# Perceiver attention by pairs of batches: scores, exponentials, turns and copies in half slots

## The chip, the cores and the metric

The kernel runs on one core of one Trainium2 chip. The metric is the device time of one execution in microseconds (us). The time before is the median of three runs, 2326.81 us (2326.65 to 2334.06).

## What is computed

The program is one block of a network with eight layers over x, 32 batches of 128 rows of 128 numbers, all in float32. The change touches the fifth layer (layer 4), an attention of the perceiver kind. Each batch attends to 128 context rows (of 96 numbers) and to its own 128 rows, with 2 heads of 64:

```python
xn = layernorm(x, ln_x_g, ln_x_b)            # x: the context here
ln = layernorm(latents, ln_l_g, ln_l_b)      # latents: layernorm of the resident x
q = ln @ Wq.T
kv = jnp.concatenate([xn @ Wkv.T, ln @ Wlkv.T], axis=1)
k, v = (kv[..., :INNER], kv[..., INNER:])
qn = rmsnorm(q, qn_g) * SCALE                # per head
kn = rmsnorm(k, kn_g)
attn = jnp.einsum('bhid,bhjd->bhij', qn, kn)
attn = jnp.where(full_mask[:, None, None, :], attn, -jnp.finfo(attn.dtype).max)
attn = jax.nn.softmax(attn, axis=-1)
out = jnp.einsum('bhij,bhjd->bhid', attn, v)
out = out.transpose(0, 2, 1, 3).reshape(b, m, INNER)
return out @ Wo.T + bo                       # times tanh(gate), added to x
```

## The kernel before

The layers run one after another with a barrier between them; x stays in SBUF (`x_resident`). Layer 4 is `layer4_perceiver` (line 1656). Its 32 batches go in 8 groups of G = 4. Each engine has its own program, a loop over slots t from -4 to 8, written out, and executes it strictly in the order of the text; semaphores with counts hold the engines together. In slot t the groups are at different steps: group t+4 has its statistics taken, t+3 is normalised and turned (work bank, copied out by ScalarE, ACT), t+2 is projected to q, k and v (`project`, lines 1951 to 1959, kept by `keep`, 1863) and squared (`square`, 1869), t+1 has its mean squares, roots (GpSimd, POOL, 1731 and 1733), scaled keys (1773) and its q, k_lat and k_ctx turned, t has scores (1961), mask, maximum and shift (`mask_scores`, 1779) and exponentials (`exponentiate`, 1887), and t-1 has its probabilities turned (1943), copied (1856), weighed with v (1975), scaled by the sums (1803), turned, mixed with wo (2024) and added to x (`update`, 1811).

PSUM is full: `score_bank` is four banks of 512 columns, in which both the scores of a group and later its turned probabilities lie (batch b's turned probabilities in bank b, a pair's scores in two banks, one for each head); `project_bank` is two, `work_bank` and `out_bank` one each. Before the change, `scores(t)` waits until all four turned probabilities of t-1 are copied, `mask_scores(t)` does both halves of the scores and then both maxima and gives one shift, and `exponentiate(t)` does the eight exponentials (two heads, four batches) at the end of ACT's slot. TensorE (PE) turns the probabilities first in slot t+1. VectorE (DVE) begins a slot by the reciprocal of the sums (1801), which waits for the exponentials, and the mean squares (1761), which wait for `square`.

## Time and profile before

| | |
|---|---|
| median of 3 runs | 2326.81 us |
| profiled execution, time | 2330.86 us |
| profiled execution, span | 2329.1 us |
| PE, DVE, ACT, POOL busy over the span | 87%, 68%, 54%, 34% |
| layer 4 in the trace | about 1358.7 to 1577.0 us |
| busy in layer 4: PE, DVE, ACT, POOL | 160.3, 115.8, 120.4, 69.1 us |

The profile is of one execution. Busy time is the time in which an engine executes; register, branch and semaphore instructions don't count. Matmuls are pipelined, so their rows overlap and their sum overstates the work: a step from one start to the next tells more. The granted clock is that of PE, 1.00 for 2.4 GHz and 0.50 for 1.2. The timeline merges like instructions that follow each other into one row.

### The profile page before, as it was taken

What the parts mean: (1) busy time and instruction counts of PE and PEld (TensorE: products, weight loads), DVE (VectorE), ACT (ScalarE), POOL (GpSimd) and SP (SyncE); (2) the same over time, 40 slices, a digit from 0 to 9 for tenths busy, and PEclk for the clock granted to TensorE, in tenths of its full rate; (3) what the DMA queues carried; (4) which work ended last, traced back from release to release, by engine and by line L of the source; (5) the groups of instructions that cost most, each with busy time, mean ns of one, the idle gap of its engine ahead of it and who ended that gap; (6) DMA issues with size and microseconds to landing.
All of it is one profiled execution on the core that took longest, in us unless ns stands there. A gap on an engine that the chain in (4) does not pass through costs nothing. (4 is left out here: it accounts for less than half of the span.)

```text
span 2329.1 us, 49606 instructions
## 1 busy us (share of the span) xinstructions
PE 2023.1 (87%) x18068; PEld 1531.8 (66%) x18068; DVE 1574.3 (68%) x3198; ACT 1254.5 (54%) x2840; POOL 796.4 (34%) x698
## 2 busy tenths in 40 slices
PE   6669999999996989789999967784998899999964
PEld 3359989899984666556666645664674566666654
DVE  5689999999997988645445356545465665656644
ACT  3279888888861767523332226741343566656631
POOL 1124444444461333234444443311000333333333
PEclk7579999999997999989999978985898899999975
DMA  2100000000002000055345300001000000000001
GB/s 58 42 1 8 14 9 14 15 8 15 13 3 76 9 9 5 16 111 112 73 96 124 74 18 11 1 1 52 1 0 11 1 4 5 5 5 5 1 2 37
DMA packets 41414, 61.75 MB, mean 27 GB/s; under 512 B 9464, under 2 KB 18208, under 8 KB 40800
## 3 DMA queue, kind: packets, MB, share of 16 engines
q1 hardware_dynamic: 41184, 58.66, 10.4%
q8 instruction: 148, 2.42, 0.4%
q14 instruction: 82, 0.67, 0.1%
HBM read 56.02 MB, written 2.62 MB: 25 GB/s over the span
## 5 line engine op out<-in xcount | busy, mean ns | idle before, releaser
L827 POOL TENSOR_TENSOR a_probs<-a_probs,a_rsums 128x1024 f32<-128x1024 f32 x64 | 121.3, 1896 | 322.6 <-DVE a_rsums L875 322.6
L1504 POOL TENSOR_TENSOR f_h<-f_gated,f_w_spread 128x512 f32<-128x512 f32 x128 | 161.6, 1268 | 196.8 <-DVE f_gated L1558 93.8
L1558 DVE TENSOR_TENSOR f_gated<-f_silu,f_up 128x512 f32<-128x512 f32 x128 | 87.2, 686 | 184.4 <-PE f_up L1635 169.8
L2330 ACT ACTIVATE f_combine<-f_logits,f_neg_row_max 128x128 f32<-128x128 f32 x512 | 198.4, 395 | 0.5 <-DVE f_neg_row_max L2188 0.5
L1598 ACT ACTIVATE f_silu<-f_gate 128x512 f32<-128x512 f32 x128 | 76.2, 597 | 222.7 <-PE f_gate L1635 220.3
L2149 POOL TENSOR_TENSOR f_slot_sum<-f_slot_sum,f_logits 128x512 f32<-128x512 f32 x96 | 122.6, 1277 | 182.7 <-DVE f_slot_max L2267 94.8
L1650 PEld LDWEIGHTS f_acc<-f_down,f_h 128*128 128x128 f32 x1024 | 129.5, 192 | 42.0 <-issue 37.2
L2157 POOL TENSOR_TENSOR f_acc<-f_acc,f_row_factor 128x512 f32<-128x512 f32 x128 | 136.3, 1066 | 60.6 <-DVE f_slot_max L2267 38.5
L2391 PE MATMUL f_give_bank<-f_y,f_combineT 128*128 128x128 f32 x1024 | 140.1, 280 | 12.1 <-DVE f_y L2237 7.5
L863 DVE TENSOR_REDUCE a_negmax<-a_score_bank 128x8 f32<-128x1024 f32 x64 | 78.2, 1223 | 103.4 <-PE a_score_bank L1004 103.4
L2380 PE MATMUL f_slot_bank<-f_logits,f_xn 128*128 128x128 f32 x1024 | 137.4, 277 | 6.4 <-issue 5.4
L2418 PE MATMUL f_logit_bank<-f_phi,f_xT 128*128 (+1 forms) x1024 | 137.6, 280 | 3.8 <-ACT f_logits L2310 3.8
L2391 PEld LDWEIGHTS f_give_bank<-f_y,f_combineT 128*128 128x128 f32 x1024 | 125.2, 193 | 19.8 <-DVE f_y L2237 13.4
L1635 PE MATMUL f_gate<-f_xT,f_gate_up 128*128 128x512 f32 x256 | 134.7, 608 | 2.1 <-DVE f_gated L1558 2.0
L2253 DVE TENSOR_TENSOR f_logits<-f_logits,f_neg_slot_max 128x512 f32<-128x512 f32 x128 | 132.5, 1035 | 4.0 <-ACT f_combine L2330 3.4
L1650 PE MATMUL f_acc<-f_down,f_h 128*128 128x128 f32 x1024 | 132.4, 276 | 2.0 <-POOL f_h L1504 2.0
L1635 PE MATMUL f_up<-f_xT,f_gate_up 128*128 128x512 f32 x256 | 131.9, 597 | 0.0
L2380 PEld LDWEIGHTS f_slot_bank<-f_logits,f_xn 128*128 128x128 f32 x1024 | 125.3, 193 | 8.2 <-issue 6.7
L2418 PEld LDWEIGHTS f_logit_bank<-f_phi,f_xT 128*128 128x128 f32 x1024 | 127.6, 197 | 4.4 <-ACT f_logits L2310 4.3
L2368 PE MATMUL f_expert_bank<-f_w,f_slots 128*32 128x128 f32 x4096 | 127.5, 276 | 1.2 <-issue 1.2
L2368 PEld LDWEIGHTS f_expert_bank<-f_w,f_slots 128*32 128x32 f32 x4096 | 109.6, 111 | 9.5 <-issue 1.9
L931 ACT ACTIVATE a_probs<-a_probs 128x1024 f32<-128x1024 f32 x64 | 67.8, 1060 | 72.3 <-DVE a_probs L866 72.3
(325 smaller groups left out, 5044.7 us busy)
## 6 DMA issues: line engine op xcount, KB each, us to landing
f_w_spread<-f_routing_rows SPq DMA_DIRECT2D x64, 512.0 KB, 10.1
f_w<-in_f_w SPq DMA_DIRECT2D x16, 256.0 KB, 2.5
a_cT<-in_ctxT SPq DMA_DIRECT2D x16, 192.0 KB, 2.5
f_gate_up<-in_f_guT SPq DMA_DIRECT2D x1, 2048.0 KB, 7.9
out<-x_resident SPq DMA_DIRECT2D x8, 256.0 KB, 2.4
c_cT<-in_ctxT SPq DMA_DIRECT2D x8, 192.0 KB, 2.4
a_ctx<-in_ctx SPq DMA_DIRECT2D x8, 192.0 KB, 2.5
f_phi<-in_f_phi SPq DMA_DIRECT2D x1, 1024.0 KB, 5.3
```

What stands on the lines that cost most here:

```text
L827: nc.gpsimd.tensor_tensor(probs[:, u], probs[:, u], rsums[:, u, :].unsqueeze(2).to_broadcast([S, 8, S]), ALU.mult).then_inc(normalised, 1)
L1504: nc.gpsimd.tensor_tensor(h[:, u % KEPT, :], gated[:, u % 2, :], w_spread[:, u // PER, u % PER, :], ALU.mult).then_inc(weighted, 1)
L1635: nc.tensor.matmul(ps[step % 2][:, :], gu_w[:, step, k, :], norm.xT[:, s, :], start=True, stop=True).then_inc(done, 1)
L1650: last = nc.tensor.matmul(acc[s][:, j * D:(j + 1) * D], h[:, u % KEPT, j * S:(j + 1) * S], down_w[:, u, :], start=u == 0 and j == 0, stop= ...
L2149: nc.gpsimd.tensor_tensor(slot_sum[:, :, :], slot_sum[:, :, :] if g > 1 else raw[:, (m - 1) % RING], raw[:, m % RING], ALU.add).then_inc(p ...
L2157: nc.gpsimd.tensor_tensor(acc[:, group(g), :], acc[:, group(g), :], factor[:, m // GROUPS % 3, group(g)].unsqueeze(2).to_broadcast([S, G, D]),
L2253: nc.vector.tensor_tensor(e, e, wide(neg_slot[:, m // GROUPS % 3, :]), ALU.add).then_inc(shifts, 1)
L2330: last = nc.scalar.activation(back[:, m % BACKS, j, :], raw[:, m % RING, j, :], ACT.Exp, bias=neg_row[:, k, b:b + 1], accum_out=row_part[: ...
L2368: last = nc.tensor.matmul(expert_banks[m % 2][rows, j * D:(j + 1) * D], slots[:, m % KEPT, j, rows], w_s[:, k, e, :], start=True, stop=True)
L2380: last = nc.tensor.matmul(slot_bank[:, j * CH:(j + 1) * CH], xn[:, g * G + j, :], raw[:, m % RING, j, :], start=True, stop=True)
L2391: last = nc.tensor.matmul(give_banks[m % 2][:, j * D:(j + 1) * D], backT[:, m % TURNED, j, :], y[:, m % KEPT, j, :], start=True, stop=True)
L2418: last = nc.tensor.matmul(logit_banks[m % 2][:, j * CH:(j + 1) * CH], xT[:, g * G + j, :], phi_c[:, c, :], start=True, stop=True)
```

## The change

Layer 4 alone is changed. Scores, mask, maximum, shift, exponentials, turned probabilities, their copies and the weighing go by pairs p of batches (0 and 1, 2 and 3), each pair with its own two banks. Pair 0 goes through to the copied probabilities within slot t; pair 1 has its scores and mask late in slot t, and its exponentials at the start of ACT's slot t+1. The order of nearly everything in PE's and ACT's slots changes, as the diff shows; DVE masks pair 0 right after the mean squares and pair 1 after the scaled keys, and normalises the context before the latent. The reciprocal of the sums moves behind them. POOL does the key roots first without the wait for the shift, the query roots then wait for all exponentials of t-1, and the context's roots move behind the bias add. The conversion of the mask moves from the start of slot -1 to the end of slot -2.

```diff
@@ POOL
                         pool.wait_ge(ms_done, j + 1)
-                        if j >= 2:
-                            pool.wait_ge(shift_ready, j - 1)
                         nc.gpsimd.tensor_tensor(rn[:, j % 2, 2 * G:], ms[:, 2 * G:], core.minus_half[:, 0:4 * G],
                                                 ALU.pow).then_inc(k_roots, 1)
+                        if j >= 2:
+                            pool.wait_ge(exps, G * (j - 1))
                         nc.gpsimd.tensor_tensor(rn[:, j % 2, 0:2 * G], ms[:, 0:2 * G], core.minus_half[:, 0:2 * G],
...
-                        n_c.gpsimd_rstd(pool, i, s, j)
                     if there(t):
                         bias.gpsimd_add(pool, at(t), n_l.xn_done)
+                    if there(t + 4):
+                        n_c.gpsimd_rstd(pool, *at(t + 4))
@@ DVE
-                def mask_scores(j):
...
+                def mask_scores(j, p):
+                    s, bs = j % 2, slice(2 * p, 2 * p + 2)
+                    dve.wait_ge(scored, 2 * j + p + 1)
+                    if j >= 2:
+                        dve.wait_ge(flips, 4 * (j - 2) + 2 * p + 2)
...
+                    nc.vector.tensor_tensor(shift[:, s, bs], negmax[:, :, bs].rearrange("p h b -> p b h"),
...
+                    if there(t + 1):
+                        mean_squares(t + 1)
+                    if there(t):
+                        if t == 0:
+                            dve.wait_ge(neg_done, 2)
+                        mask_scores(t, 0)
+                    if there(t + 3):
+                        n_c.vector_normalise(dve, *at(t + 3))
+                        n_l.vector_normalise(dve, *at(t + 3))
                     if there(t - 1):
                         invert_sums(t - 1)
...
                     if there(t + 1):
                         scale_keys(t + 1)
                     if there(t):
-                        if t == 0:
-                            dve.wait_ge(neg_done, 2)
-                        mask_scores(t)
+                        mask_scores(t, 1)
                     if there(t - 1):
                         normalise_outputs(t - 1)
@@ ACT: the slot after the change
+                        exponentiate(t - 1, 1)
                     if there(t + 1):
                         empty_work("q", t + 1, qT[:, (t + 1) % 2], scale=q_gain[:, 0:1])
+                    if there(t + 2):
+                        keep(t + 2, 0)
                     if there(t - 1):
                         copy_turned_probs(t - 1, 2)
                         copy_turned_probs(t - 1, 3)
                     if there(t + 2):
-                        keep(t + 2, 0)
+                        keep(t + 2, 1)
                     if there(t + 3):
                         empty_work("c", t + 3, cT[:, (t + 3) % 2, :], bias=vecs[0:C, 1:2], scale=vecs[0:C, 0:1])
                     if there(t + 2):
-                        keep(t + 2, 1)
+                        keep(t + 2, 2)
+                    if there(t):
+                        exponentiate(t, 0)
                     if there(t + 3):
                         empty_work("l", t + 3, lT[:, (t + 3) % 2, :], bias=vecs[:, 3:4], scale=vecs[:, 2:3])
                     if there(t + 2):
-                        keep(t + 2, 2)
+                        keep(t + 2, 3)
+                    if there(t):
+                        copy_turned_probs(t, 0)
+                        copy_turned_probs(t, 1)
...
-                    if there(t):
-                        exponentiate(t)
                     if there(t + 2):
                         square(t + 2)
@@ PE
-                def scores(j):
+                def scores(j, p):
                     s = j % 2
                     pe.wait_ge(work_emptied, use["k_ctx", j] + 1)
                     if j:
-                        pe.wait_ge(pT_done, G * j)
...
+                        pe.wait_ge(pT_done, G * (j - 1) + 2 * p + 2)
...
+                def weigh(j, p):
+                    pe.wait_ge(pT_done, G * j + 2 * p + 2)
+                    if j and p == 0:
                         pe.wait_ge(updated, j)
...
                 for t in SLOTS:
+                    if there(t):
+                        scores(t, 0)
                     if there(t - 1):
-                        turn_probs(t - 1)
+                        weigh(t - 1, 0)
                     if there(t + 1):
                         turn("q", t + 1, kept, G * (t + 1) + G, lambda b: q[:, (t + 1) % 2, b, :])
                     if there(t + 2):
                         project(t + 2, 0)
                     if there(t - 1):
-                        weigh(t - 1, 0)
-                        weigh(t - 1, 1)
+                        turn_probs(t - 1, 1)
+                    if there(t + 2):
+                        project(t + 2, 1)
                     if there(t + 3):
                         turn("c", t + 3, n_c.xn_done, t + 4, lambda b: n_c.xn[:, (t + 3) % 2, b, :], width=C)
+                    if there(t + 2):
+                        project(t + 2, 2)
                     if there(t):
-                        scores(t)
-                    if there(t + 2):
-                        project(t + 2, 1)
+                        scores(t, 1)
                     if there(t - 1):
-                        weigh(t - 1, 2)
-                        weigh(t - 1, 3)
+                        weigh(t - 1, 1)
                     if there(t + 3):
                         turn("l", t + 3, n_l.xn_done, t + 4, lambda b: n_l.xn[:, (t + 3) % 2, b, :])
                     if there(t + 2):
-                        project(t + 2, 2)
+                        project(t + 2, 3)
+                    if there(t):
+                        turn_probs(t, 0)
...
-                    if there(t + 2):
-                        project(t + 2, 3)
```

## Rows read from the trace of the kernel before

**Rows 1.** The page: busy us of each engine over the span.
```profile
PE 2023.1 (87%) x18068; PEld 1531.8 (66%) x18068; DVE 1574.3 (68%) x3198; ACT 1254.5 (54%) x2840; POOL 796.4 (34%) x698
```

**Rows 2.** Busy us by stretch: PE, weight loads, DVE, ACT, POOL; clock, DMA share, GB/s.
```profile
1358.70:1577.00 218.30, 160.32 (x896) 123.61 (x896) 115.81 (x296) 120.37 (x289) 69.13 (x49) 0.84 0.03 8
1465.41:1487.89 22.48, 18.20 (x112) 14.06 (x112) 13.73 (x36) 14.74 (x37) 7.95 (x6) 0.92 0.01 1
...
1489.30:1510.20 20.90, 16.60 (x113) 13.16 (x111) 11.38 (x19) 14.75 (x38) 5.78 (x3) 0.98 0.00 1
1424.40:1531.10 106.70, 88.45 (x554) 69.76 (x553) 61.80 (x138) 72.59 (x179) 35.38 (x24) 0.93 0.02 4
1531.10:1574.90 43.80, 34.72 (x207) 29.61 (x205) 17.36 (x21) 18.82 (x50) 6.96 (x4) 0.78 0.00 1
```

**Rows 3.** Waits of 1355 to 1580 us: total us, times, longest.
```profile
DVE a_rsum L1801 <- ACT a_scores L1892: 32.7, 8, 8.8
```

**Rows 4.** Timeline of one slot, DVE, POOL and ACT: start, us, engine, line.
```profile
1489.22 1.07 ACT L1860 ACTIVATE a_probsT<-a_score_bank 128x512 f32<-128x512 f32 x2
1489.36 1.75 DVE L1761 TENSOR_REDUCE a_ss<-a_sq 128x24 f32<-128x1536 f32 x1 [1.26 <-ACT a_sq L1875]
1491.41 2.94 POOL L1731 TENSOR_TENSOR a_rn<-a_ms,minus_half 128x16 f32<-128x16 f32 x1 [8.30 <-DVE a_ms L1766]
1494.38 1.23 DVE L1773 TENSOR_TENSOR a_kn<-a_kv,a_rn 128x1024 f32<-128x1024 f32 x1 [1.07 <-POOL a_rn L1731]
1495.52 2.35 DVE L1785 TENSOR_TENSOR a_scores<-a_score_bank,a_neg 128x1024 f32<-128x1024 f32 x2
...
1500.16 0.17 DVE L1795 TENSOR_TENSOR a_shift<-a_negmax,a_rn 128x8 f32<-128x8 f32 x1
1502.76 0.28 ACT L1865 ACTIVATE a_q<-a_project_bank 128x128 f32<-128x128 f32 x1 [0.43 <-PE a_project_bank L1958]
1503.41 0.69 ACT L1885 ACTIVATE a_kT<-a_work_bank,a_vecs 128x512 f32<-128x512 f32 x1
1503.98 0.61 ACT L1892 ACTIVATE a_scores<-a_scores,a_shift,a_rn 128x256 f32<-128x256 f32 x1
1508.65 0.62 ACT L1873 ACTIVATE a_sq<-a_q 128x512 f32<-128x512 f32 x1
```

**Rows 5.** Timeline, PE: steps at full clock, and the scores at half clock (last).
```profile
1453.33 1.89 PE L1981 MATMUL a_out_bank<-a_kv,a_probsT 128*128 128x64 f32 x16
1455.06 0.61 PE L1940 MATMUL a_work_bank<-ident,a2l_xn 128*128 128x128 f32 x4
1455.50 0.81 PE L1957 MATMUL a_project_bank<-a_w_lat,a2l_xT 128*128 128x384 f32 x2
...
1456.63 0.63 PE L1940 MATMUL a_work_bank<-ident,a_kn 128*128 128x128 f32 x4
...
1459.62 1.06 PE L2024 MATMUL a_out_bank<-a_wo,a_oT 128*128 128x128 f32 x8
...
1514.32 2.00 PE L1971 MATMUL a_score_bank<-a_kT,a_qT 64*128 64x256 f32 x16
...
1535.23 3.79 PE L1971 MATMUL a_score_bank<-a_kT,a_qT 64*128 64x256 f32 x16
```

**Rows 6.** Timeline: the squares that end slots -1, 0, 5, and the last update.
```profile
1399.32 1.07 ACT L1875 ACTIVATE a_sq<-a_kv 128x1024 f32<-128x1024 f32 x1
1423.33 1.04 ACT L1875 ACTIVATE a_sq<-a_kv 128x1024 f32<-128x1024 f32 x1
1530.04 1.05 ACT L1875 ACTIVATE a_sq<-a_kv 128x1024 f32<-128x1024 f32 x1
1574.11 0.75 DVE L1816 SCALAR_TENSOR_TENSOR x_resident<-a_out_bank,gates,x_resident 128x512 f32<-128x512 f32 x1 [2.67 <-PE a_out_bank L2024]
```

**Rows 7.** Busy by stretch, columns as in rows 2: clock after a stretch of waits.
```profile
1557.67:1561.08 3.41, 0.66 (x4) 0.42 (x4) 2.11 (x4) 0.52 (x2) 0.00 (x0) 0.91 0.00 0
1561.08:1564.50 3.42, 3.29 (x15) 3.29 (x16) 0.75 (x1) 3.42 (x13) 0.00 (x0) 0.50 0.00 0
```

More of the change, by code:

```diff
@@ L1803, in normalise_outputs @@
                 def normalise_outputs(j):
[L1804 removed]
+                    dve.wait_ge(weighed, 2 * j + 2)
                     dve.wait_ge(sums_inverted, j + 1)
@@ L1885, in empty_work, with exponentiate @@
                     nc.scalar.activation(out, ps, ACT.Identity if "bias" in args else ACT.Copy, **args).then_inc(work_emptied, 1)
-                def exponentiate(j):
+                def exponentiate(j, p):
                     s = j % 2
-                    act.wait_ge(shift_ready, j + 1)
-                    for b in range(G):
+                    act.wait_ge(shift_ready, 2 * j + p + 1)
+                    for b in (2 * p, 2 * p + 1):
                         for h in range(H):
@@ L1941, in turn, with turn_probs @@
                     last.then_inc(work_turned, 1)
-                def turn_probs(j):
-                    for b in range(G):
+                def turn_probs(j, p):
+                    for b in (2 * p, 2 * p + 1):
                         pe.wait_ge(exps, G * j + b + 1)
@@ L1964, in scores @@
                     if j:
-                        pe.wait_ge(pT_done, G * j)
-                    for p in range(2):
-                        for b in (2 * p, 2 * p + 1):
-                            for h in range(H):
-                                r = slice(DH * h, DH * h + DH)
-                                first = 512 * (2 * p + h) + 256 * (b % 2)
-                                last = nc.tensor.matmul(score_bank[:, first:first + 256], qT[r, s, b, :],
-                                                        kT[r, s, b].rearrange("p c k -> p (c k)"), start=True, stop=True)
-                        last.then_inc(scored, 1)
@@ L1975, in weigh @@
-                def weigh(j, b):
-                    pe.wait_ge(pT_done, G * j + b + 1)
-                    if j and b == 0:
-                        pe.wait_ge(updated, j)
-                    for h in range(H):
-                        for c in range(2):
-                            last = nc.tensor.matmul(out_bank[:, (b * H + h) * DH:(b * H + h + 1) * DH], pT[:, b, 2 * h + c, :],
-                                                    kv[:, j % 4, b, c, 1, h * DH:(h + 1) * DH], start=c == 0, stop=c == 1)
-                    if b == G - 1:
-                        last.then_inc(weighed, 1)
+                        pe.wait_ge(pT_done, G * (j - 1) + 2 * p + 2)
@@ new lines, in scores @@
+                    for b in (2 * p, 2 * p + 1):
+                        for h in range(H):
+                            r = slice(DH * h, DH * h + DH)
+                            first = 512 * (2 * p + h) + 256 * (b % 2)
+                            last = nc.tensor.matmul(score_bank[:, first:first + 256], qT[r, s, b, :],
+                                                    kT[r, s, b].rearrange("p c k -> p (c k)"), start=True, stop=True)
+                    last.then_inc(scored, 1)
+                def weigh(j, p):
+                    pe.wait_ge(pT_done, G * j + 2 * p + 2)
+                    if j and p == 0:
+                        pe.wait_ge(updated, j)
+                    for b in (2 * p, 2 * p + 1):
+                        for h in range(H):
+                            for c in range(2):
+                                last = nc.tensor.matmul(out_bank[:, (b * H + h) * DH:(b * H + h + 1) * DH],
+                                                        pT[:, b, 2 * h + c, :], kv[:, j % 4, b, c, 1, h * DH:(h + 1) * DH],
+                                                        start=c == 0, stop=c == 1)
+                    last.then_inc(weighed, 1)
@@ L2015, in _ @@
                         last.then_inc(o_turned, 1)
-                    if there(t + 2):
-                        project(t + 2, 3)
                     if there(t + 1):
```

43 lines of the change are left out of this document (13 added, 30 removed).

## Prediction

> **What bounds the kernel now.** I first read the page's busy shares [rows 1]: TensorE (PE) looks nearly full over the whole span, but the change touches only the perceiver attention, about 1358.7 to 1577.0 us. The busy table of that stretch [rows 2] is the one to read: in 218.3 us PE is busy 160.3, ScalarE (ACT) 120.4, VectorE (DVE) 115.8, GpSimd (POOL) 69.1. So no engine is full, and the stage is set by a chain. A slot is one round of the program order over t; I cut slots at the end of the two squares, the last thing ACT does in each. Slots 1 to 5 take 1424.37 to 1531.09, 106.7 us or 21.3 each; slot 0 takes 24.0; what follows slot 5, up to the last update, 43.8 [rows 6].
>
> The waits show one link of the chain [rows 3]: DVE's reciprocal waits for the exponentials (32.7 us, 8 times), which ends each of DVE's slots. The timeline of one slot, 1489.33 to 1510.22, shows the order [rows 4]. DVE begins when the squares end; it sums, normalises, waits until 1494.38 for POOL's roots, scales keys, masks all four batches, takes all maxima, and has the shift at 1500.16+0.17. Then it scales the outputs, PE turns them, ACT copies them and a key tile, and only at 1503.98 do all eight exponentials start, 4.67 us in a row up to 1508.65, then the squares, up to 1510.22, which release DVE again. During the exponentials PE has only turns to do, and during DVE's half of the slot ACT idles. The loop is DVE 11.0 us, hand-over and copies 3.7, exponentials and squares 6.2: 20.9.
>
> **The floors.** ACT's steps from start to start: exponentials 4.67; four keeps 0.65 each, 2.6; three key and query copies 0.57 each, 1.7; the two copies that the rows give as 0.78 long about 0.67 each (the next start comes 0.12 before an end, as for the key copy, 0.69 long), 1.3; four probability copies 1.9 (two take 0.95); output copy 0.5; squares 1.5. Sum 14.2 [rows 4]. PE's steps at full clock, from start to start [rows 5]: projection 1.13; weighing a pair 1.73; a group of four turns 0.44, of which there are six and four more for the probabilities; scores, 2.00 long, 1.92 (a pair 0.96); mixing, 1.06 long, 1.0. Sum 4x1.13 + 2x1.73 + 10x0.44 + 1.92 + 1.0 = 15.3. DVE is 11.4 to 13.7 and POOL up to 8.0 [rows 2]. So a slot can't be under about 15.3.
>
> PE's busy column for the full-clock slot says 16.60, its weight loads 13.16 [rows 2]. The Trainium skill (Perfetto Trace Analysis, Identifying the Most-Contended Engine) says that matmul occupancy is no measure of nearness to the limit, since matmuls are pipelined, and that weight-load occupancy is one. By the first column the floor would be 16.6 and five slots could give at most 23.5 us; by the second 13.2 and up to 40. My steps lie between, and the sum uses the steps.
>
> **The change, part by part.** (1) It takes the second pair's exponentials out of the loop. Pair 0 of batch group t is masked early in DVE's slot and exponentiated mid-slot by ACT; pair 1 is masked late and exponentiated first thing in the next slot. I worked a steady slot from the end of the k_ctx copy (0), at full clock. PE: scores(t,0) 0.05 to 1.0, weigh(t-1,0) from 1.15 (it waits for update(t-2)), query turn to 3.3, projection 0 out at 4.7, turned probabilities of pair 1 out at 5.4, projection 1 out at 6.85. ACT beside it: squares to 1.4, exponentials of pair 1 to 3.7, query copy, keep 0 to 5.35, two probability copies to 6.3, keep 1 to 7.6. DVE: sum of squares from 1.45, mask, maximum and shift of pair 0 to 6.05, context normalised at 7.1. PE: context turn 7.6, projection 2 out at 9.0, scores(t,1) to 9.8, weigh(t-1,1) to 11.5, latent turn, projection 3 out at 13.3, probabilities of pair 0 out at 14.1, k_lat turn. ACT: context copy, keep 2 to 9.7, exponentials of pair 0 to 12.0, latent copy, keep 3 to 13.9, two probability copies to 14.9, k_lat copy out at 15.6, output copy to 16.1, k_ctx copy out at 17.0. DVE has the second shift at 13.6, the scaled outputs at 14.3. Mixing ends at 17.3 and the update at 18.1, and the next weigh waits for it some 0.1. So a slot is 17.1 us. What is late next is the ping-pong between PE's projections and ACT's keeps; PE then works 15.3 of 17.1. Slot 5 has no context or latent turn and comes to 16.2. Slots 1 to 5: 106.7 - (4x17.1 + 16.2) = 22.1 us saved.
>
> (2) Slot 0 loses its wait from first scores to a late exponential. From k_ctx out at 1398.9 the same walk, with the clock half for a spell round 1407 and 1.28 us of table load, ends at 1417.1, its squares at 1418.5 against 1424.37: 5.9 saved.
>
> (3) The tail. Slot 6 has no projections: exponentials (5,1) to 2.3 after slot 5's squares, scores(6,1) 4.0 to 5.0, second shift 8.95, outputs turned 10.3, k_ctx out 11.5, update 12.8. Slot 7: exponentials (6,1) 11.5 to 13.9; PE first does scores(7,0), then weigh(6,0), which waits for update(5), to 14.6; turned probabilities out 15.5, copies 16.2, scores(7,1) 17.2, weigh 18.9, shift 20.0, output 20.7, update 23.9. Slot 8: weigh(7,0) waits for that update, 25.6; turns, copies, weigh(7,1) 29.1; last update 33.1, against 43.8: 10.7 saved.
>
> (4) More instructions: DVE has two shifts where it had one, and each maximum now waits for its own mask. Before, two masks took 2.35 from 1495.52 [rows 4], the maxima as long, and the last shift ended at 1500.33: 4.8 us. A pair now is half of 2.35, half of 2.35 again, 0.17 and three completions of about 0.05 to 0.1: 2.7, so 5.4 instead of 4.8 us, so +0.6 us of DVE a slot; DVE stays the third engine, so 0, and 0.6 a slot (4 us in all) if it became the bound.
>
> (5) POOL. The query roots now wait for the exponentials of t-1. Behind that wait are the latent's roots, the bias and the context's roots. The exponentials are done at 3.7, before the key roots end (3.5+2.9), so nothing. The context's roots go behind the bias add, 1.27 us later: ready about 16.8 and wanted at 23.1, so nothing. The added waits of the probability copies and of the masks are on work a slot or two old: nothing. No DMA is added; the context load is released by the context's normalisation, up to 1.9 us later in the slot, and has a slot to land. The mask's conversion (2.26 us) stays between slots -2 and -1: 0. None of (5) can gain but the key roots, which no longer wait for the old shift; that wait was never last.
>
> (6) The clock. All these steps are at 2.4 GHz (granted 1.0). The whole stage had 0.84 and the tail 0.78 [rows 2]; the same scores took 3.79 us at 1.2 GHz, 2.00 at 2.4 [rows 5]. PE's clock fell after stretches in which it waited for exponentials or for DVE: 0.66 us busy of 3.41, then 0.50 granted [rows 7]. Such stretches leave the steady slots, so I take them at full clock, and two spells of about 3.4 us for the tail, each costing 1.7: -3.4.
>
> **Sum.** 22.1 + 5.9 + 10.7 - 3.4 = 35.3 us. The profiled execution's span is 2329.1 and its time 2330.9; the median of the runs is 2326.8, 4.1 lower. 2326.8 - 35 = 2292.
>
> The Trainium skill (TensorE: Matmul & The Clock Gate, HAM oscillation) tells of a kernel whose PE waits between bursts and is throttled again each time. By that the denser PE here keeps or gains clock; the order of falls in this trace agrees.
>
> **Rivals.**
> - Hand-overs longer than I walked. A slot has about eight PE-ACT exchanges in series; 0.2 us more on each is 1.6 a slot, 18.7, and the stage saves 27: 2300. For: every step is read where its cover was different. Against: the gaps in the rows are 0.03 to 0.08 us.
> - The half clock stays, one spell of 3.4 us in each of six slots: with PE the bound each costs its full 1.7, 10 in all, saves 25: 2302. For: from 11.8 to 16 PE has mostly turns and short waits. Against: its longest wait is under 1 us.
> - Slower. PE at the half clock for most of the time. It has 15.3 us of work a slot and was covered by the loop; now it is the bound. A fraction h of half-clock time stretches a slot to about 17.1/(1-h/2); it passes 21.3 at h = 0.39 and is slower by over 0.3% only when five slots lose 16 + 7 us, 25.9 each, at h = 0.68, as slot 0 and the tail save 16. At h = 0.8 slots 1 to 5 lose 36, less the 16: 2347. For: h was 2 x 0.16 = 0.32 over the stage [rows 2]. Against: it was 2 x 0.07 = 0.14 in slots 1 to 5 [rows 2].
> - The pairs don't come apart: a late second shift holds ACT's first exponentials, and the loop is DVE plus exponentials as before. It needs the shift over 4.9 us later than I have it (13.6 against 18.5). Slots stay 20 to 21: 2318.
> - PE's floor is reached, 15.3 a slot: 9 us more saved, 2283.
>
> **Chances.** Forecast 0.55, longer hand-overs 0.18, spells 0.10, floor 0.08, pairs together 0.06, slower 0.03. Measurement of this kernel can tell about 0.3%, 7 us. Faster by more than that takes all but the last and some of the pairs-together case: 0.92; same 0.05; slower 0.03. Both ends of the range are those of the rivals: the floor case, 2283, and spells with a little of both, 2305.
>
> **What would show it.** DVE's reciprocals 17.1 us apart, which were 22.48 in one slot [rows 2] and 21.3 in the mean; DVE's wait for the exponentials at the reciprocal near nothing; PE's wait for exponentials under 10 us in sum; granted clock of the steady slots above 0.95; exponentials in groups of four; the last update about 39 us earlier in the stage. The prediction is wrong if the slots stay near 21, or if PE's granted clock in them falls under 0.85.

## Result, and the profile of the changed kernel

The changed kernel takes 2299.86 us, the median of 4 runs (2296.99 to 2301.6); the kernel before took 2330.43 (2326.65 to 2335.53) in runs beside them. The ratio is 0.9859, with an interval of 0.9839 to 0.9879. The direction and the range of the prediction held, and its value, 2292, was 7.9 too low: 3.6 of it because before was slower in these runs than the 2326.8 that I subtracted from, and the rest because 30.6 us were saved where 35 were forecast. The profiled executions are 2298.30 us (span 2296.1) and 2330.86 (span 2329.1), so 33.0 us of span are to be placed.

Totals hardly move, as the page's busy line shows beside [rows 1]: the same matmuls, eight more instructions on DVE.

```profile
PE 2007.8 (87%) x18068; PEld 1517.7 (66%) x18068; DVE 1575.6 (69%) x3206; ACT 1256.2 (55%) x2840; POOL 801.1 (35%) x698
```

The windows of layer 4 (columns as in [rows 2]) are cut like those of before, at the end of the squares. They are slot 0, slot 1, a steady slot, slot 5, what follows it, and the whole stage.

```profile
1398.40:1417.60 19.20, 13.73 (x59) 8.45 (x57) 12.53 (x34) 12.51 (x27) 8.89 (x6) 0.80 0.05 12
1417.60:1438.20 20.60, 19.44 (x116) 15.70 (x115) 13.95 (x37) 14.94 (x37) 8.90 (x6) 0.86 0.04 10
...
1455.70:1473.20 17.50, 16.54 (x114) 12.98 (x114) 13.86 (x37) 15.02 (x38) 8.90 (x6) 1.00 0.00 1
...
1490.70:1507.80 17.10, 15.49 (x106) 12.19 (x106) 9.75 (x12) 13.46 (x36) 5.74 (x3) 1.00 0.00 1
1507.80:1543.50 35.70, 27.03 (x208) 23.32 (x207) 18.18 (x24) 20.61 (x57) 6.98 (x4) 0.94 0.00 1
1358.60:1545.60 187.00, 146.90 (x896) 111.61 (x896) 117.84 (x304) 121.90 (x289) 73.89 (x49) 0.89 0.04 9
```

In a steady slot PE is busy 16.54 of 17.50 us at full clock; before it was 16.60 of 20.90. The work is the same and 3.4 us of waiting are gone. The second thing to see is the clock column: 0.80 and 0.86 in slots 0 and 1, then 1.00, and 0.94 at the end.

Slots are read off the squares on ACT's timeline, as in [rows 6]; here those that end slots -1, 0 and 1, and the last two updates on DVE's.

```profile
1397.34 1.05 ACT L1875 ACTIVATE a_sq<-a_kv 128x1024 f32<-128x1024 f32 x1
1416.54 1.04 ACT L1875 ACTIVATE a_sq<-a_kv 128x1024 f32<-128x1024 f32 x1
1437.20 1.05 ACT L1875 ACTIVATE a_sq<-a_kv 128x1024 f32<-128x1024 f32 x1
...
1531.88 0.75 DVE L1814 SCALAR_TENSOR_TENSOR x_resident<-a_out_bank,gates,x_resident 128x512 f32<-128x512 f32 x1 [2.66 <-PE a_out_bank L2028]
...
1542.79 0.75 DVE L1814 SCALAR_TENSOR_TENSOR x_resident<-a_out_bank,gates,x_resident 128x512 f32<-128x512 f32 x1 [3.69 <-PE a_out_bank L2028]
```

The table of slots, made in the same way for each kernel in it (us, one profiled execution each), is what most of the rest rests on. The tail runs from the end of slot 5 to the end of the last update. The kernel names are those of the experiments below; "changed, a later run" is the changed kernel once more, unedited.

| kernel | -1 | 0 | 1 | 2 | 3 | 4 | 5 | tail |
|---|---|---|---|---|---|---|---|---|
| before | 14.50 | 23.98 | 21.24 | 21.23 | 22.49 | 20.89 | 20.87 | 43.77 |
| changed | 11.37 | 19.19 | 20.67 | 17.49 | 17.49 | 17.50 | 17.09 | 35.72 |
| changed, a later run | 11.38 | 17.68 | 17.40 | 17.49 | 17.49 | 17.49 | 17.10 | 39.75 |
| e1_pairs_old_order | 14.19 | 22.89 | 21.68 | 21.71 | 21.69 | 21.34 | 21.32 | 45.97 |
| e2_small_parts | 13.16 | 21.83 | 21.31 | 21.29 | 21.31 | 20.85 | 20.86 | 43.88 |
| e3_exp_at_end | 11.37 | 21.51 | 20.67 | 21.06 | 21.11 | 21.02 | 17.11 | 39.79 |
| e4_pool_old | 11.37 | 18.12 | 20.67 | 17.50 | 17.49 | 17.49 | 17.09 | 36.47 |
| e5_half_weigh | 11.36 | 17.87 | 18.66 | 16.26 | 16.26 | 16.26 | 15.71 | 36.67 |
| e7_reorder | 15.71 | 18.18 | 17.22 | 17.72 | 17.72 | 17.72 | 16.81 | 39.61 |
| e8_fill_clock | 11.37 | 17.69 | 17.42 | 17.49 | 17.50 | 17.50 | 17.09 | 39.43 |
| e9_scores_first | 11.37 | 17.01 | 21.19 | 17.19 | 17.18 | 17.19 | 16.08 | 36.06 |
| e10_tail_bank | 11.36 | 17.70 | 20.67 | 17.49 | 17.49 | 17.49 | 17.10 | 31.61 |
| e11_all | 11.37 | 20.04 | 17.13 | 17.19 | 17.18 | 17.19 | 16.08 | 31.60 |

Where the 33.0 us lie: slots 1 to 5 went from 106.7 to 90.2 (16.5), slot 0 gave 4.8, the tail 8.05, slot -1 gave 3.1 of which the slots ahead of it took back 1.2; that is 31.2. The other 1.8 lie outside layer 4, in code that wasn't touched.

The waits of 1355 to 1545 us (total, times, longest) no longer show [rows 3]: DVE's reciprocal waits for exponentials only once by name, 0.29 us in the last slot. Behind POOL's wait for DVE's mean squares, which heads the list as it did before (52.3 us, 78.6 before), now stand waits of engines for PE.

```profile
DVE x_resident L1814 <- PE a_out_bank L2028: 25.4, 8, 4.3
ACT a_q L1865 <- PE a_project_bank L1960: 24.8, 30, 2.6
...
PE a_work_bank L1942 <- ACT a_kT L1885: 6.4, 7, 1.6
```

That DVE's own wait is gone proves little, since the reciprocal has moved behind other work. More telling is PE's wait for the exponentials, in the stage before and in the changed one:

```profile
PE a_score_bank L1947 <- ACT a_scores L1892: 19.8, 26, 3.6
```

```profile
PE a_score_bank L1949 <- ACT a_scores L1892: 0.2, 1, 0.2
```

The timeline of a steady slot, from one first pair of scores to the next (17.49 us), in the rows of PE with two of ACT and one of DVE:

```profile
1454.41 1.13 PE L1972 MATMUL a_score_bank<-a_kT,a_qT 64*128 64x256 f32 x8
1455.48 1.99 PE L1983 MATMUL a_out_bank<-a_kv,a_probsT 128*128 128x64 f32 x16
1455.64 0.59 ACT L1892 ACTIVATE a_scores<-a_scores,a_shift,a_rn 128x256 f32<-128x256 f32 x1
1457.31 0.61 PE L1942 MATMUL a_work_bank<-ident,a_q 128*128 128x128 f32 x4
...
1458.83 1.04 PE L1949 MATMUL a_score_bank<-ident,a_scores 128*128 128x128 f32 x8
...
1459.85 0.91 PE L1959 MATMUL a_project_bank<-a_w_lat,a2l_xT 128*128 128x384 f32 x2
...
1461.33 0.64 PE L1942 MATMUL a_work_bank<-ident,a2c_xn 128*96 128x128 f32 x4
...
1462.05 0.91 PE L1959 MATMUL a_project_bank<-a_w_lat,a2l_xT 128*128 128x384 f32 x2
...
1462.21 0.19 DVE L1799 RECIPROCAL a_rsum<-a_prob_sums 128x8 f32<-128x8 f32 x1
...
1463.33 1.14 PE L1972 MATMUL a_score_bank<-a_kT,a_qT 64*128 64x256 f32 x8
...
1464.09 0.60 ACT L1892 ACTIVATE a_scores<-a_scores,a_shift,a_rn 128x256 f32<-128x256 f32 x1
...
1464.39 2.00 PE L1983 MATMUL a_out_bank<-a_kv,a_probsT 128*128 128x64 f32 x16
...
1470.42 0.63 PE L1942 MATMUL a_work_bank<-ident,a_kn 128*128 128x128 f32 x4 [0.75 <-ACT a_kT L1885]
...
1471.90 1.14 PE L1972 MATMUL a_score_bank<-a_kT,a_qT 64*128 64x256 f32 x8
```

The exponentials stand in two groups, from 1455.64 and from 1464.09, where [rows 4] had all eight in one. PE goes through its list almost without a stop. Taking each start minus the one before, and the plain step of the same group as the work, four gaps are left: 0.14 before projection 1, 0.30 before the context's turn, 0.28 before projection 2, and 0.91 before the k_ctx turn, which has to wait until ACT has copied k_lat out of the one work bank. That is 1.6 us of gaps and 15.9 of work.

### The profile page after: what moved, and what is told of

Same layout as the page of the kernel before. It is cut to its first block and busy times, and to the rows that moved or that the text cites. A ratio compares the mean times of both kernels' runs of the same rounds, so it can differ in the third digit from the quotient of the medians.

```text
span 2296.1 us, 49636 instructions
## 1 busy us (share of the span) xinstructions
PE 2007.8 (87%) x18068; PEld 1517.7 (66%) x18068; DVE 1575.6 (69%) x3206; ACT 1256.2 (55%) x2840; POOL 801.1 (35%) x698
```

## Experiments

Kernels run together share their runs of the kernel before. Where a kernel has a single time, it is that of one execution, and its slots carry the verdict.

**Half the change: pairs without the new order** on PE, ACT and DVE; POOL keeps its new one.

```diff
 # PE, ACT, DVE: the pair functions, called in the order of before
-                        weigh(t - 1, 0)
+                        turn_probs(t - 1, 0)
+                        turn_probs(t - 1, 1)
...
-                        exponentiate(t - 1, 1)
...
+                        exponentiate(t, 0)
+                        exponentiate(t, 1)
```

> The changed kernel's functions by pairs (two banks, two masks, maxima and shifts, two weighings), called pair after pair at the old places of the old order, with the new GpSimd order. Theory A, the gain is that the second pair's exponentials left the loop: the slots stay at 20.9 to 21.3 us and grow by the 0.6 us of the second shift and the two completions, so 2330 to 2335, 0 to 4 us above the kernel before. Rival B, the pairs' own banks and finer waits give the gain by themselves: slots near 18 to 19, 2305 to 2315.

Measured: 2335.6 us, ratio 1.0011 (0.9997 to 1.0025). DVE's old wait is back, 31.7 us against 32.7 in [rows 3]:

```profile
DVE a_rsum L1799 <- ACT a_scores L1891: 31.7, 8, 8.3
```

Splitting the operations gains nothing by itself and costs about 0.45 us a slot (21.32 against 20.87 in slot 5); in this order DVE is in the loop, so the extra work of term (4) shows, at 0.45 where I had estimated 0.6. The gain is not in the split, then, but in the order.

**The small parts alone**, on the kernel before: POOL's order, the context normalised first, the reciprocal later, the mask's conversion earlier.

```diff
-                    if there(t - 1):
-                        invert_sums(t - 1)
                     if there(t + 1):
                         mean_squares(t + 1)
                     if there(t + 3):
-                        n_l.vector_normalise(dve, *at(t + 3))
                         n_c.vector_normalise(dve, *at(t + 3))
+                        n_l.vector_normalise(dve, *at(t + 3))
+                    if there(t - 1):
+                        invert_sums(t - 1)
```

> The kernel before with the small parts alone: key roots without the old wait, query roots behind all exponentials of the group before, context roots behind the bias add, context normalised before the latent, reciprocal behind them, mask conversion at the end of slot -2. Theory A: 0 within 2 us (one of the traces gained 3.1 us in slot -1, where the context comes first, and lost 1.1 in slot -2; so -2 at most). Rival C, the small parts carry a third of the gain: -8 to -12 us.

Measured: 2327.51, ratio 0.9971 (0.9956 to 0.9987), 5 us less than the kernel before beside it. I had missed that. Slots 1, 2, 4 and 5 are within 0.1 of before; what differs in the traces is slot -1 (13.16 against 14.50), slot 0 (21.83 against 23.98) and slot 3 (21.31 against 22.49). In slot 3 both have about the same share of half clock (clock 0.90 here, 0.92 before), but before has a spell in mid-slot and this kernel at the slot's ends. So these parts help while the pipeline fills; how much of slots 0 and 3 is theirs one trace can't tell, as the clock's spells move between executions of one kernel (see the filler below). What each of the four does was not separated by a run.

This run also shows what DVE's wait for the exponentials is worth as a sign. With the reciprocal moved it is nearly gone, PE's stays, and so do the slots (waits of 1355 to 1575 us):

```profile
PE a_score_bank L1948 <- ACT a_scores L1893: 17.2, 21, 3.6
...
DVE a_rsum L1802 <- ACT a_scores L1893: 4.4, 2, 2.7
```

**Only the moved exponential undone**: the changed kernel with pair 1's exponentials back at the end of ACT's slot.

```diff
-                    if there(t - 1):
-                        exponentiate(t - 1, 1)
...
                         empty_work("k_ctx", t + 1, kT[:, (t + 1) % 2, :, CTX, :], scale=vecs[:, 5:6])
+                    if there(t):
+                        exponentiate(t, 1)
```

> The changed kernel with the exponentials of pair 1 moved back to the end of ACT's slot, ahead of the squares. Theory A: the squares and with them DVE's mean squares, the first shift and the context's normalisation come 2.3 us later; PE's context turn slips by about 1.8, so slots of 19.3 instead of 17.5 and 8 to 11 us more than the changed kernel, 2308 to 2311. Rival D, PE's own work sets the slot and covers this: slots stay at 17.5, 2300.

Measured: 2321.48 (2312.21 to 2334.77), ratio 0.9948 (0.9927 to 0.997), some 20 us over the changed kernel, about double what I expected. PE's timeline shows a wait of 2.46 us where the changed kernel has none by this row in its steady slots, and after it the same eight score matmuls at half clock, 2.08 us, where those of 10 us later take 1.13; the slot's window has clock 0.92 (columns as above).

```profile
1447.25 0.64 PE L1942 MATMUL a_work_bank<-ident,a2c_xn 128*96 128x128 f32 x4 [2.46 <-DVE a2c_xn L147]
...
1449.40 2.08 PE L1972 MATMUL a_score_bank<-a_kT,a_qT 64*128 64x256 f32 x8
...
1459.06 1.13 PE L1972 MATMUL a_score_bank<-a_kT,a_qT 64*128 64x256 f32 x8
...
1441.66:1462.72 21.06, 17.85 (x113) 13.74 (x112) 14.07 (x37) 15.01 (x37) 8.90 (x6) 0.92 0.04 11
```

The slot is 21.06 instead of 17.49. From start to start, the gap before the context's turn is 2.63 where it was 0.30, and the gap of 0.28 before projection 2 closes: 2.1 of the 3.57 is waiting. Projection 2, the scores and the weighing behind it step 1.5 more at half clock. So in slots 2 to 4 this one move carries nearly the whole steady gain, somewhat more than half of it as waiting and the rest as clock that the waiting would lose. In slot 5, which has no context's turn, the move is worth nothing: 17.11 with it undone, 17.09 in the changed kernel, 20.87 before. There the rest of the order gives the gain. Of the 20 us about 4 are the tail's (39.79 for 35.72), which the unedited kernel shows too in its later run. The Trainium skill (TensorE: Matmul & The Clock Gate, HAM oscillation) tells of such a kernel, in which PE pauses between bursts and is throttled again each time; here one row shows the pause and the next ones the throttle, once in each of slots 2 to 4.

**POOL's order undone.** The wait stands ahead of the key roots again; it is for all exponentials of the group before, where the kernel before waited for that group's shift.

```diff
+                        if j >= 2:
+                            pool.wait_ge(exps, G * (j - 1))
                         nc.gpsimd.tensor_tensor(rn[:, j % 2, 2 * G:], ms[:, 2 * G:], core.minus_half[:, 0:4 * G],
                                                 ALU.pow).then_inc(k_roots, 1)
-                        if j >= 2:
-                            pool.wait_ge(exps, G * (j - 1))
...
+                        n_c.gpsimd_rstd(pool, i, s, j)
                     if there(t):
                         bias.gpsimd_add(pool, at(t), n_l.xn_done)
-                    if there(t + 4):
-                        n_c.gpsimd_rstd(pool, *at(t + 4))
```

> The changed kernel with GpSimd's old order: the wait ahead of the key roots (on all exponentials of the group before), context roots ahead of the bias add. Theory A: the exponentials of pair 1 end 2.3 us after the squares and the mean squares end 1.9 after them, so the key roots start about 0.4 us later and still end ahead of the scaled keys; 0 within 1 us, slots 17.5. Rival C: 2 us or more slower.

Measured: 2303.38, ratio 0.9861 (0.9841 to 0.9882), the changed kernel's own, and its slot -1 and steady slots are the same to 0.01. Term (5) at nothing is shown for POOL's part.

**How near PE is to being the bound.** Half of the weighing is left out, then in another kernel the squares of the keys after the first group.

```diff
-                            for c in range(2):
+                            for c in range(1):
...
-                                                        start=c == 0, stop=c == 1)
+                                                        start=True, stop=True)
```

> The changed kernel with half of the weighing left out (only the latent half of v, so its output leaves out the context's share): 1.8 us less of TensorE work in each slot. Theory P, PE's own work sets the slot of 17.5: slots of 15.7 to 16. Theory Q, the slot is a chain through ACT and DVE at which PE waits (the context's turn waits for squares, mean squares, mask, maximum, shift and normalisation; the k_ctx turn waits for ACT's copies): the first weighing's cut is swallowed by the wait for the context, the second's gives about 0.5, slots of 16.9 to 17.2.

```diff
-                    dve.wait_ge(squares, 2 * j + 2)
+                    dve.wait_ge(squares, j + 2)
...
-                    nc.scalar.activation(sq[:, G * D:].rearrange("p (n d) -> p n d", d=D),
...
+                    if j == 0:
+                        nc.scalar.activation(sq[:, G * D:].rearrange("p (n d) -> p n d", d=D),
```

> The changed kernel with the squares of the keys left out after the first group (its key norms are then those of group 0): 0.95 us less of ACT in each slot, at a place where PE doesn't wait. Theory P (PE's work sets the slot): 0. Theory Q (the chain from the squares to the context's turn): DVE starts 0.95 earlier; since keep 1 is ready only 0.1 after the context, 0.1 to 0.3 less a slot, and DVE waits longer for the second scores.

Measured, half weighing: 2296.35 in one execution, steady slots 16.26, between my two forecasts: 1.24 less for 1.8 us less of PE's work. The rest went into longer waits on DVE and ACT. From start to start the gap before the context's turn is 0.81 where it was 0.30, and that before projection 1 is 0.49 where it was 0.14; on PE's timeline the turn now has a wait:

```profile
1459.22 0.64 PE L1942 MATMUL a_work_bank<-ident,a2c_xn 128*96 128x128 f32 x4 [0.64 <-DVE a2c_xn L147]
```

Measured, key squares left out: 2295.90 in one execution, updates 17.49 to 17.50 us apart, as in the changed kernel, with 1.05 us less of ACT's work a slot. Two of them on DVE's timeline:

```profile
1448.53 0.75 DVE L1814 SCALAR_TENSOR_TENSOR x_resident<-a_out_bank,gates,x_resident 128x512 f32<-128x512 f32 x1 [2.84 <-PE a_out_bank L2029]
1466.03 0.75 DVE L1814 SCALAR_TENSOR_TENSOR x_resident<-a_out_bank,gates,x_resident 128x512 f32<-128x512 f32 x1 [3.11 <-PE a_out_bank L2029]
```

So ACT has slack at the end of its slot, and PE gives two thirds of what is taken from it: the bound is PE with short exchanges in between, not PE alone. The Trainium skill (Perfetto Trace Analysis, Identifying the Most-Contended Engine) calls matmul occupancy a poor measure of nearness to the limit and points to the share of peak arithmetic and to weight loads. Here weight loads are 12.98 of 17.50, 74%, and by them a quarter of the slot would be free, while the slot followed two thirds of what was taken from PE. The sum of steps, 15.9 of 17.5, was the better reading.

**Filling PE's gaps by another order.** Two attempts. The first normalises the context ahead of the mask, turns it ahead of projection 1, and puts projection 3 behind the k_lat turn.

```diff
 # PE alone; DVE and ACT follow
                         turn_probs(t - 1, 1)
+                    if there(t + 3):
+                        turn("c", t + 3, n_c.xn_done, t + 4, lambda b: n_c.xn[:, (t + 3) % 2, b, :], width=C)
                     if there(t + 2):
                         project(t + 2, 1)
-                    if there(t + 3):
-                        turn("c", t + 3, n_c.xn_done, t + 4, lambda b: n_c.xn[:, (t + 3) % 2, b, :], width=C)
...
-                    if there(t + 2):
-                        project(t + 2, 3)
...
+                    if there(t + 2):
+                        project(t + 2, 3)
```

> The changed kernel with three steps moved: DVE normalises the context ahead of the first mask; PE turns the context ahead of projection 1 and ACT copies it ahead of keep 1; projection 3 and keep 3 go behind the k_lat turn and its copy. Theory Q: PE's waits at the context (0.7 us in sum with the keeps) and ahead of the k_ctx turn (0.75) are filled, slots of 16.6 to 16.9 instead of 17.5, 3 to 5 us off the changed kernel, 2296. Theory P would give the same only down to PE's floor, 16.5. Rival R, the moved steps open other waits (keep 1 and keep 2 back to back with no PE work between them): slots of 17.5 or more, no gain.

Measured: 2303.42, ratio 0.9859 (0.9837 to 0.9881); steady slots 17.72, so 0.2 longer, and slot -1 is 15.71 where it was 11.37, which was not traced further. The waits at the turns are gone and two others have come, on PE's timeline:

```profile
1462.78 0.91 PE L1960 MATMUL a_project_bank<-a_w_lat,a2l_xT 128*128 128x384 f32 x2 [0.85 <-ACT a_kv L1867]
...
1471.58 1.16 PE L2029 MATMUL a_out_bank<-a_wo,a_oT 128*128 128x128 f32 x8 [0.47 <-ACT a_oT L1927]
```

Two projections next to each other need the two halves of the project bank emptied in a row. The second attempt leaves the projections apart: context first on DVE, and scores of pair 1 ahead of projection 2.

```diff
-                    if there(t + 2):
-                        project(t + 2, 2)
                     if there(t):
                         scores(t, 1)
+                    if there(t + 2):
+                        project(t + 2, 2)
```

> The changed kernel with two steps moved: DVE normalises the context ahead of the first mask, and PE does the second pair's scores ahead of projection 2, so that work stands between projection 1 and projection 2 while ACT keeps the first. Theory: PE's wait for keep 1 (0.6 us with the context's wait) is covered, slots of 16.8 instead of 17.5. Rival: the second exponentials' pair or the k_ctx turn, which hang on ACT, are late next: slots of 17.3 to 17.5.

Measured: 2301.15 in one execution; steady slots 17.19, 0.3 less, where I expected 16.8. The gaps before the context's turn and before projection 2 are closed, the 0.14 before projection 1 stays, and the wait at the k_ctx turn grew from 0.75 to 1.13:

```profile
1470.56 0.60 PE L2021 MATMUL a_out_bank<-ident,a_o 128*128 128x128 f32 x4
1472.29 0.63 PE L1943 MATMUL a_work_bank<-ident,a_kn 128*128 128x128 f32 x4 [1.13 <-ACT a_kT L1886]
```

What PE gains ahead of it, it hands back at the k_ctx turn, which stands for ACT's k_lat copy, itself behind keep 3 and two probability copies.

**The clock of the start.** Eight matmuls of no use, in slot 0, where PE is idle most.

```diff
+                def filler(columns, n, done):
+                    pe.wait_ge(masked, done)
+                    for _ in range(n):
+                        nc.tensor.matmul(score_bank[:, columns:columns + 256], core.ident[:, :], wl[:, 0:256], start=True, stop=True)
...
+                    if t == 0:
+                        filler(0, 3, 1)
```

> The changed kernel with eight matmuls of 128x256 that write to score banks nobody reads any more, in slot 0, where PE waits: three ahead of the context's turn, three ahead of the k_ctx turn, two behind it. Theory H, the clock falls at 1403.8 and 1417.5 because PE waited in the stretch before: both spells go, slot 1 is 17.5 instead of 20.7 and slot 0 1 us shorter, 3 to 5 us off, 2296. Rival: the falls do not hang on these waits: slots 0 and 1 stay at 19.2 and 20.7 or grow by the added work, 2300 to 2303.

Measured: 2301.24, ratio 0.9855 (0.983 to 0.9879), no gain. Slots 0 and 1 came to 17.69 and 17.42, which looks like success, but the tail was at half clock from 1531.6 and took 39.43. The changed kernel run again, with nothing edited, did the same: 2300.87, ratio 0.9863 (0.9837 to 0.9889). Its windows for slot 0, slot 1, the tail, and the tail's last part (columns as above):

```profile
1405.30:1423.00 17.70, 11.18 (x62) 6.94 (x61) 12.44 (x34) 12.50 (x28) 8.90 (x6) 1.00 0.05 12
1423.00:1440.40 17.40, 16.43 (x113) 12.88 (x113) 13.87 (x37) 15.01 (x37) 8.91 (x6) 1.00 0.05 11
1509.96:1549.70 39.74, 31.08 (x208) 27.09 (x207) 18.22 (x24) 20.70 (x57) 6.98 (x4) 0.82 0.00 1
1537.00:1549.70 12.70, 9.69 (x42) 8.41 (x41) 1.43 (x2) 1.79 (x3) 0.00 (x0) 0.50 0.00 0
```

So the filler did nothing that can be shown. In its two profiled executions the unedited kernel pays for spells once in slots 0 and 1 and once in the tail: slots 0 and 1 together are 39.86 and 35.08 (4.8 less), the tails 35.72 and 39.75 (4.0 more). It needn't be one or the other: e3's trace is slow in all three. Nor is the profiled execution the median: these two took 2298.30 and 2308.21, the later one the longest of its four. Layer 4 was the shorter one in it (183.5 us against 184.9, from its first statistics to its last update), and some 11 us lie in layers that no kernel here changes.

**The tail.** In it each weighing waits for the update before, as both use `out_bank`. No projection runs there, so the last group's output goes to a project bank, with its exponentials, weighing and turns a slot earlier.

```diff
+        out_of = lambda j: project_bank[:, 0:512] if j == LAST else out_bank[:, :]
...
+                    if t == LAST:
+                        exponentiate(t, 1)
...
-                    if j and p == 0:
+                    if j == LAST and p == 0:
+                        pe.wait_ge(kept, G * GROUPS)
+                    elif j and p == 0:
                         pe.wait_ge(updated, j)
...
+                    if t == LAST:
+                        weigh(t, 0)
+                        turn_probs(t, 1)
```

> The changed kernel with the last group's output in the projection bank, which is free by then; weigh(7,0) no longer waits for update(6), the last exponentials go ahead of the output copy of group 6, and PE turns the last probabilities and mixes group 6 in the waits. Theory: the tail is a chain through update(6) and the one output bank: 35.7 becomes 32.5 us, the steady slots stay at 17.5. Rival: the tail hangs on the clock alone: 35.7 to 39.4 as before.

Measured: 2291.01 in one execution; tail 31.6 against 35.72 (I expected 32.5). The last group is weighed while the group before is turned and mixed, and its update follows 5.1 us after that group's, where it was 10.9:

```profile
1525.73 1.90 PE L1989 MATMUL a_project_bank<-a_kv,a_probsT 128*128 128x64 f32 x16
...
1529.51 0.75 DVE L1816 SCALAR_TENSOR_TENSOR x_resident<-a_out_bank,gates,x_resident 128x512 f32<-128x512 f32 x1 [4.33 <-PE a_out_bank L2037]
...
1534.64 0.75 DVE L1816 SCALAR_TENSOR_TENSOR x_resident<-a_project_bank,gates,x_resident 128x512 f32<-128x512 f32 x1 [2.66 <-PE a_project_bank L2037]
```

**All three together**: the second order, the filler and the tail's bank.

> Scores ahead of projection 2, the last group's own bank, and the eight matmuls that fill slot 0's waits, together. By the sums: 0.7 us in each of five slots, 3.2 in the tail, 4.7 in slots 0 and 1, of which the clock may take back 3 to 4 in the tail: 5 to 11 us less than the changed kernel, 2290 to 2296, ratio to the kernel before 0.981 to 0.984. Rival: given back at the clock, 0.986.

Measured: 2293.72 (2291.63 to 2295.48), ratio 0.9832 (0.981 to 0.9855). Steady slots are 17.19, slot 5 is 16.08, the tail 31.6, and slot 0, at 20.04, has the spell again. It is 7 us below the changed kernel run beside it (2300.87, 2300.07 to 2308.21), the best of the kernels with more than one time; the two ratios' intervals overlap at their edges (0.9837 to 0.9855), so the size of that step is loose.

## Why the prediction held, and where it was off

**The bound and the loop** were read rightly. The slots stood at 21 by a chain through DVE and all eight exponentials. In the changed order they come to 17.5 and PE's wait for exponentials is 0.2 us instead of 19.8. e1 and e3 show from both sides that the order does it and not the split. Two things I had not seen. DVE's wait at the reciprocal, which I read the loop from (32.7 us in [rows 3]), was a poor sign: e2 brings it to 4.4 by moving the reciprocal, and its slots stay. And what ties the late exponentials to the slot in e3 is PE's wait for the context's turn, so that slot 5 escapes it.

**Part (1), slots 1 to 5: 22.1 forecast, 16.5 measured.** Of the 5.6 missing, slot 1 is 3.6 (20.67 for 17.1), the three next ones 0.4 each, and slot 5 0.9 (17.09 for 16.2). In the steady slot I had 15.3 of PE's work and 1.8 of gaps; it has 15.9 and 1.6. So the walk's gaps were right and the term mis-sized is PE's steps. A pair's scores step 1.07, where I took half of 1.92, 0.96. A pair's weighing steps 1.83 when it follows scores and 1.73 when it follows a projection, as it did in [rows 5] and does in e9 (1465.99 to 1467.72). The scores thus add 0.2 to the slot and the weighings 0.2. The four projections together add 0.1 (4.63 for 4.52): after a gap one steps 0.75 + 0.43, not 0.65 + 0.43. I had halved a group that was measured whole, and took its neighbours' steps from another order.

**Part (2), slot 0: 5.9 forecast, 4.8 measured.** I had put a spell of half clock there, round 1407, and there was one, from 1403.8. In the later run of the same kernel, with clock 1.00, the slot was 17.68 long, 6.3 less than before, so what the miss hangs on is the clock.

**Part (3), the tail: 10.7 less 3.4 of clock forecast, 8.05 measured.** The last spell cost little more than the mixing at 2.07 us instead of 1.16, about 1.0, so the work itself gave 9.05 instead of 10.7. The last three updates end 13.1, 24.8 and 35.7 after slot 5's squares, where the walk had 12.8, 23.9 and 33.1. The three rounds were 0.3, 0.6 and 1.7 longer than I had them, and 1.0 of the last is the spell. The mechanism stands: weigh(7,0) waited 1.00 for the update, and e10, which took away the shared bank, gave 4.1, of which about 1.0 is that spell (its tail ran at clock 1.00).

**Part (4)**, 0.6 of DVE a slot at no cost: the split costs 0.45 where DVE is in the loop (e1), and in the changed order DVE is busy 13.9 of 17.5.

**Part (5)** at nothing was right for the steady slots (e4 for POOL, e2 for the rest) and wrong for the start: slots up to -1 gave 1.9 that I had put at 0, and e2's trace gave 4.5 from slot -1 on, 3.5 of it in slots -1 and 0. I had asked what each moved operation delays and not what it brings forward: in slot -1 the context's turn comes when DVE has normalised the context, which is now earlier. PE's timeline of before, and then of the changed kernel, has it so:

```profile
1389.92 1.09 PE L1940 MATMUL a_work_bank<-ident,a2c_xn 128*96 128x128 f32 x4 [3.85 <-DVE a2c_xn L147]
```

```profile
1390.03 0.64 PE L1942 MATMUL a_work_bank<-ident,a2c_xn 128*96 128x128 f32 x4 [0.38 <-DVE a2c_xn L147]
```

The stall of 3.85 us is gone, and with it the half clock behind it (1.09 us for four turns, 0.64 now). Counted from the end of slot -2's squares, the turn starts at 4.03 in before and in e1, which keep the latent first, and at 3.01 in e2 and in the changed kernel, which put the context first. So of the four small parts this one brings PE's turn 1.0 forward, of the 1.34 that e2 gains in that slot; the changed order of PE, which now has projection 1 ahead of the turn, goes on to 11.37. What e2 gains in slot 0 was not traced to one part.

**Part (6), the clock**: size nearly right, place mostly wrong, and the size partly by luck, since another execution of the kernel has its spells elsewhere. I had 3.4 us in the tail; the profiled execution has a spell of 6.8 us at 1417.5 in slot 1 (20.67 where the later run has 17.40, so 3.3) and 1.0 in the tail, 4.3. The two windows of slots 0 and 1 in which the clock fell:

```profile
1403.80:1410.60 6.80, 6.61 (x22) 4.27 (x23) 4.91 (x17) 4.10 (x9) 4.35 (x3) 0.55 0.12 29
...
1417.50:1424.30 6.80, 6.80 (x31) 5.87 (x30) 6.58 (x15) 3.35 (x12) 4.53 (x2) 0.56 0.01 2
```

**The sum.** 16.5 + 4.8 + 8.05 + 1.9 is 31.2 in the stage against 35.3, and 1.8 outside it bring the span to 33.0. The 1.9 and the 1.8 I had put at nothing; without them the saving would be 29.3, so the nearness of the total is in part luck. The prediction's marks: reciprocals and updates 17.49 apart (said 17.1), steady clock 1.00 (said above 0.95), exponentials by four (so), PE's wait for exponentials 0.2 (said under 10), last update 31.2 us earlier from the stage's start (said 39, too much).

**The rivals.** Longer hand-overs: no, gaps were shorter than walked. Half clock in every slot: not in the changed kernel, but e3 shows that it is one 2.46 us stall away. Pairs that don't come apart: no, though e3's 21.1 is that rival's slot, by another wait. Its 2318 had no sum beside it: with slots of 20 to 21 and the rest as forecast it would be about 2309. The bound of 23.5 us that I gave for five slots of 16.6 should be 23.7. The floor of 15.3: not reached; e9 without its last gap would be at about 16.1 (17.19 less 1.13), an estimate.

## What to carry to other kernels

When a chain runs DVE, ACT, DVE once a round and no engine is full, split the batch of work in two and let the second half's step start the next round: here the gain was in the order, and the split alone cost a little. Take a split group's step from a row with the new neighbour in front of it: scores, weighings and projections stepped about 0.1 us longer behind some neighbours than behind others, and that was the whole error of the steady slot's work. Don't take a wait's leaving the list for a gain, when the edit has moved the instruction that waited. Read a reorder of the fill and the drain separately from the steady rounds: here they held nearly half of the gain, and in the drain a further bank gave 4 us more when two new orders of the steady slot gave 0.3 each round at best.

## What the runs showed of the hardware

A wait of 2.46 us before one turn was followed by PE at 1.2 GHz in each of slots 2 to 4 of e3, some 3.4 us of a slot by its clock of 0.92, while waits of up to 1.13 us (e9) never had this behind them in steady slots. Between them lies the wait of 2.00 us ahead of slot 0's context's turn. In one execution of the changed kernel half clock follows it (four turns take 1.09 us), in the other full clock (0.64):

```profile
1403.99 1.09 PE L1942 MATMUL a_work_bank<-ident,a2c_xn 128*96 128x128 f32 x4 [2.00 <-DVE a2c_xn L147]
```

```profile
1410.89 0.64 PE L1942 MATMUL a_work_bank<-ident,a2c_xn 128*96 128x128 f32 x4 [2.00 <-DVE a2c_xn L147]
```

What I had not expected is that the fall at the start isn't fixed by the program: the same kernel had 0.80 and 0.86 in slots 0 and 1 in one execution and 1.00 in both in another, there with PE busy only 11.18 of 17.70 us, and then paid in the tail (0.82 against 0.94). The medians of the two sets of runs differ by 1.0 us. What decides where the spell falls was not found, and it means that a single profile can't credit an edit with the clock of those slots.
